# A memory layer's running sums as VectorE scans along the tokens, batch by batch, with the token dispatch interleaved

## The chip, the cores and the metric

The kernel runs on one core of a Trainium2 chip. The metric is the device time of one execution in microseconds. Engine names in the rows: PE is TensorE (PEld its weight loads), DVE is VectorE, ACT is ScalarE, POOL is GpSimd, SP is SyncE, which here only issues DMAs.

## What is computed

The input is `x` of 4 batches, 1024 tokens, 128 channels, in float32. Two layers follow each other, each with a residual and a layer norm.

```
z = x @ W_in                       # memory channels 128 + 32, query channels 256
z_mem = causal depthwise conv, 4 taps, of the first 160 channels
p   = exp(clip(score_scale * z_mem[128:160]) + log weight of the position)     # (b, l, 32)
phi = z_mem[0:128] * theta         # 32 heads k, 4 h, 8 m = 1024 features a token
num = cumsum over tokens of p * (cos phi, sin phi);  den = cumsum of p
y   = sum over m of num * query / max(den, 1e-4);  y = silu(y scaled) @ W_out
x1  = layernorm(x + y)
out = layernorm(x1 + sum over the 2 best of 8 experts of weight * mlp_e(x1) + mlp_shared(x1))
mlp(x) = square(relu(x @ w_up)) @ w_down       # 128 -> 512 -> 128
```

The cosine and sine of 4096 tokens by 1024 features, their weighting by `p`, their running sum over the tokens and the product with the query are the bulk of the first layer.

## The kernel before

**Memory stage.** A unit is 128 tokens of one batch, the tokens on the partitions; there are `NT` = 32 units, and unit `i` belongs to batch `i % 4`. `phases(i)` (L604) forms 1024 phases in PSUM; ScalarE rounds them (`rounding`, L383), VectorE takes the fraction (`fraction`, L748), ScalarE makes `Abs` and two sines (L387, L390, L394); the result is `feat`, 2 halves of 1024 columns. GpSimd multiplies each half by `p` (`weigh`, L495). The running sum within a unit is a matmul with the triangular matrix `tri` (`sums`, L620: 4 matmuls of 512 columns); what comes from the unit before of the same batch is carried by copying the last rows out of PSUM (`last_row`, L403) and adding them with an accumulating DMA into row 0 of the next `feat` (`carry`, L503). VectorE multiplies the sums with the query (`read_out`, L769) and reduces over `m` (L778, L787, L795). `value` (L543) is the convolution as 4 matmuls, `queries` (L590) the query projection.

**Dispatch stage.** It works on groups of 512 tokens, `NG` = 8 of them: transposing and projecting y (L938, L948), residual and statistics (`residual`, L1238 to L1246), `normalise`, transposing x1 (L959), router logits (`route`, L969), `choose` (L1266 to L1279), `rank`, `place` and `count` (each token's slot in the table), 8 indirect DMAs on GpSimd that write 128 rows each into the table in DRAM (`scatter`, L1192), and the shared MLP: `up` (L998, 4 matmuls of 512 columns a group), `relu` and `square` (L1116, L1122), `down` (L1008, 16 matmuls of 128 columns). Only the first group's front part runs beside the last units; the order of all of it is written out by hand in `rest()` of each engine.

**Routed and finish stages.** `routed` loads 46 tiles from the table (L1468), transposes them (L1488) and runs the experts' MLPs (L1500, L1513); `finish` adds, normalises and stores.

A float32 matmul leaves two MATMUL records in the trace (L620: 128 matmuls, 256 records); a transpose leaves one. Each engine executes its program in order and waits on semaphores in place.

## Time and profile before

| | us |
|---|---|
| median of 3 runs | 490.81 |
| lowest, highest run | 489.8, 494.01 |
| span of the profiled execution | 498.7 |
| PE busy in it | 453.9 |
| DVE busy | 356.7 |
| ACT busy | 354.5 |
| POOL busy | 315.1 |

The profiled execution's span is 7.9 us above the median of the runs. Busy times are sums over the whole span; the stages differ, so they are read by stretch. A granted clock (PEclk) of 1.00 is the higher of TensorE's two levels, 2.4 GHz, and 0.50 the lower, 1.2 GHz; values between are means over a stretch.

### The profile page before, as it was taken

The page shows a single profiled execution, that of the slowest core. Times are in us where ns is not written, and L with a number is a line of the kernel's source. Part 1 is how long each engine was busy: PE and PEld are TensorE (multiplying, and loading weights), DVE is VectorE, ACT ScalarE, POOL GpSimd, SP SyncE. Part 2 cuts the span into 40 slices and gives each one's busy share as a digit, 9 for nine tenths or more (in the row PEclk, how much of TensorE's full clock was granted, in tenths as well). Part 3 has the DMA queues.
Part 4 walks back from the last instruction along what each step waited for, and adds up shares of the span by engine and source line. Part 5 has one row for each costly group of instructions (what it writes and reads, how often), then busy time and mean ns, then how long its engine had stood idle before and what let it go on. Part 6 is the DMA issues. An engine that isn't in the chain of part 4 may idle for free.

```text
span 498.7 us, 7644 instructions
## 1 busy us (share of the span) xinstructions
PE 453.9 (91%) x2184; PEld 293.6 (59%) x2184; DVE 356.7 (72%) x873; ACT 354.5 (71%) x557; POOL 315.1 (63%) x285
## 2 busy tenths in 40 slices
PE   8997999999999988798898898489999999999983
PEld 5332444444344333455576675389999999899721
DVE  5898999999999999998688964353333333455246
ACT  3989999999999999815455555327667667566537
POOL 4754789999999999845566666604555455555421
PEclk9998999999999999989799999979999999999997
DMA  8031246654343434001111111131222222222095
GB/s 274 8 122 43 86 146 213 216 196 151 130 153 131 151 133 148 3 1 33 39 45 43 45 43 47 46 94 51 72 65 81 71 60 58 60 57 67 11 324 182
DMA packets 41193, 48.56 MB, mean 97 GB/s; under 512 B 5616, under 2 KB 25266, under 8 KB 41152
## 3 DMA queue, kind: packets, MB, share of 16 engines
q1 hardware_dynamic: 35792, 39.07, 23.8%
q0 software_dynamic: 5216, 8.70, 5.6%
q8 instruction: 18, 0.29, 0.2%
q10 hardware_dynamic: 144, 0.31, 0.2%
q14 instruction: 23, 0.19, 0.1%
HBM read 19.17 MB, written 29.11 MB: 97 GB/s over the span
## 4 chain that ended last, share of the span: by engine, by line
PE 40%; POOL 22%; DVE 16%; issue 8%; ACT 7%; DMA 2%; another core or an unknown queue 2%; DVEq 0%; POOLq 0%; SPq 0%; ACTq 0%
POOL memory_feat L495 17%; PE routed_ph L1500 13%; PE routed_po L1513 12%; PE dispatch_sph L998 4%; PE dispatch_spo L1008 3%; POOL memory_feat L503 2%; DVE memory_prod L769 2%; DVE memory_y_raw L778 2%; POOL memory_prod L518 2%; PE memory_nsum L620 1%; ACT finish_xo L1714 1%; PE routed_px L1488 1%; PE dispatch_plr L969 1%; DVE memory_feat L769 1%
## 5 line engine op out<-in xcount | busy, mean ns | idle before, releaser
L495 POOL TENSOR_TENSOR memory_feat<-memory_feat,memory_p_tok 128x1024 f32<-128x1024 f32 x64 | 125.9, 2063 | 17.1 <-ACT memory_feat L390 14.2
L620 PE MATMUL memory_nsum<-memory_feat,tri 128*128 128x512 f32 x256 | 118.1, 604 | 6.3 <-ACT memory_last_rows L403 2.4
L1476 POOL DMA_INDIRECT pick_scratch<-routed_ob,routed_xg x71 | 71.6, 1008 | 75.1 <-DVE routed_ob L1597 56.7
L1192 POOL DMA_INDIRECT table_scratch<-dispatch_xrow,dispatch_slot x64 | 61.9, 967 | 40.9 <-PE dispatch_sph L998 18.9
L620 PEld LDWEIGHTS memory_nsum<-memory_feat,tri 128*128 128x128 f32 x256 | 47.8, 192 | 65.1 <-issue 56.2
L1546 ACT ACTIVATE routed_rel<-routed_ph 128x512 f32<-128x512 f32 x71 | 42.3, 597 | 47.7 <-PE routed_ph L1500 46.7
L1513 PE MATMUL routed_po<-routed_w2c,routed_hid 128*128 128x128 f32 x568 | 71.3, 276 | 1.2 <-DVE routed_ob L1597 0.7
L1500 PE MATMUL routed_ph<-routed_xs,routed_w1c 128*128 128x256 f32 (+1 forms) x368 | 71.1, 337 | 1.2 <-DVE routed_w2c L1583 0.9
L1597 DVE TENSOR_SCALAR routed_ob<-routed_po,routed_xg 128x128 f32<-128x128 f32 x71 | 22.6, 347 | 69.2 <-issue 49.6
L769 DVE TENSOR_TENSOR memory_prod<-memory_nsum,memory_query 128x1024 f32<-128x1024 f32 x58 | 68.8, 1216 | 1.9 <-PE memory_nsum L620 1.8
L1513 PEld LDWEIGHTS routed_po<-routed_w2c,routed_hid 128*128 128x128 f32 x568 | 67.0, 192 | 1.9 <-issue 1.1
L1500 PEld LDWEIGHTS routed_ph<-routed_xs,routed_w1c 128*128 128x128 f32 x368 | 56.5, 191 | 6.2 <-ACT routed_xs L1537 1.8
L403 ACT COPY memory_last_rows<-memory_nsum 32x1024 f32<-32x1024 f32 x56 | 54.2, 1005 | 3.5 <-DVE memory_prod L769 2.6
L1116 ACT ACTIVATE dispatch_srel<-dispatch_sph 128x512 f32<-128x512 f32 x32 | 19.1, 596 | 38.4 <-PE dispatch_sph L998 29.8
L1008 PE MATMUL dispatch_spo<-w,dispatch_shid 128*128 128x128 f32 x256 | 36.0, 295 | 8.2 <-ACT dispatch_shid L1122 8.2
L1008 PEld LDWEIGHTS dispatch_spo<-w,dispatch_shid 128*128 128x128 f32 x256 | 34.4, 209 | 14.4 <-ACT dispatch_shid L1122 8.6
L1555 ACT ACTIVATE routed_hid<-routed_rel 128x512 f32<-128x512 f32 x71 | 42.5, 638 | 0.0
L748 DVE SCALAR_TENSOR_TENSOR memory_feat<-memory_feat,memory_ph 128x1024 f32<-128x1024 f32 x32 | 38.7, 1209 | 5.3 <-ACT memory_feat L383 4.5
L787 DVE TENSOR_REDUCE memory_y_raw<-memory_prod 128x96 f32<-128x1536 f32 x24 | 41.8, 1741 | 0.0
L604 PE MATMUL memory_ph<-setup_th_f,setup_k_val 64*128 64x512 f32 x128 | 36.8, 651 | 4.4 <-DVE memory_feat L748 4.4
L394 ACT ACTIVATE memory_feat<-memory_feat,memory_half_pi 128x1024 f32<-128x1024 f32 x32 | 36.5, 1140 | 0.0
L998 PE MATMUL dispatch_sph<-dispatch_x1T,w 128*128 128x512 f32 x64 | 35.0, 636 | 1.1 <-DVE memory_feat L769 1.1
(192 smaller groups left out, 694.6 us busy)
## 6 DMA issues: line engine op xcount, KB each, us to landing
table_scratch<-memory_blank SPq DMA_DIRECT2D x68, 260.0 KB, 2.6
finish_pick<-pick_scratch SPq DMA_DIRECT2D x16, 256.0 KB, 6.0
routed_xg<-table_scratch SPq DMA_DIRECT2D x25, 130.0 KB
w<-w_up SPq DMA_DIRECT2D x9, 256.0 KB, 2.7
w<-w_down SPq DMA_DIRECT2D x9, 256.0 KB, 3.1
x_tok<-x SPq DMA_DIRECT2D x4, 512.0 KB, 3.7
out<-finish_xo SPq DMA_DIRECT2D x7, 256.0 KB, 2.3
routed_xg<-table_scratch SPq DMA_DIRECT2D x21, 65.0 KB
```

The lines of the kernel that those rows point to most:

```text
L403: nc.scalar.copy(last_rows[32 * b:32 * b + 32, h * NF:(h + 1) * NF], nsum[96:P, h * NF:(h + 1) * NF]).then_inc(rows_kept, 1)
L495: nc.gpsimd.tensor_tensor(v, v, pv, ALU.mult).then_inc(wfeat_done, 1)
L620: last = nc.tensor.matmul(nsum[:, o:o + 512], tri[:], feat[:, i % U, h, q * 512:(q + 1) * 512], start=True, stop=True)
L769: nc.vector.tensor_tensor(products(i)[:, h, :].rearrange("p (q r c) -> p q r c", q=KQ, r=REP), nv, qv.unsqueeze(2).broadcast_to([P, KQ, RE ...
L998: nc.tensor.matmul(sph[q % 2][:], w1[:, E, q * P:(q + 1) * P], x1T[:, g % XR].rearrange("p t c -> p (t c)"), start=True, stop=True).then_i ...
L1008: last = nc.tensor.matmul(spo[g % 2][:, t * D:(t + 1) * D], shid[:, g % 2, q, t * P:(t + 1) * P], w2[:, E, q, :], start=(q == 0), stop=(q ...
L1192: nc.gpsimd.indirect_dma_start(out=table, in_=xrow[:, r, n, :], in_offset=None, out_offset=bass.IndirectOffsetOnAxis(ap=slot[:, r, n:n + 1 ...
L1476: nc.gpsimd.indirect_dma_start(out=pick_dram, in_=ob[:, u, h, :], in_offset=None, out_offset=bass.IndirectOffsetOnAxis(ap=xg[:, t % XU, h, ...
L1500: last = nc.tensor.matmul(ph[s][:, q * n:(q + 1) * n], w1c[:, u, q * P:(q + 1) * P], xs[:, s, 0:n], start=True, stop=True)
L1513: last = nc.tensor.matmul(po[:, h * D:(h + 1) * D], hid[:, s, q * n + h * P:q * n + (h + 1) * P], w2c[:, u, q, :], start=(q == 0), stop=(q ...
L1546: nc.scalar.activation(rel[:, n % 2, :], ph[s][:, o:o + FC * P], ACT.Relu).then_inc(rel_done, 1)
L1555: nc.scalar.activation(hid[:, s, o:o + FC * P], rel[:, n % 2, :], ACT.Square).then_inc(hid_done, 1)
```

## The change

`memory` and `dispatch` become one stage, `front`. A **unit** is now one of 8 head indices `n` of one batch: 128 features on the partitions (4 query groups by 4 h by 8 m), 1024 tokens along the columns, cosine and sine as two halves. There are again 32 units (`NU`), batch by batch. The tables that `phases` multiplies have 32 rows instead of 64.

The weight `p` is no longer multiplied into the features. The sums are kept relative to the current weight: with r(t) = p(t-1)/p(t), the recurrence s(t) = r(t) s(t-1) + feature(t) is one `tensor_tensor_scan` of 1024 elements a half (`cumulated`); r is spread from 32 heads to 128 partitions by 4 matmuls of 256 columns (`broadcast`) into the single PSUM buffer `abc`, and the factor p/den is applied to the result (`scaled`). The product with the query is GpSimd's (`product`), the sum over `m` is TensorE's (`gathered`, 8 matmuls of 256 columns into 4 column groups). ScalarE applies the silu to 2 units' result and issues 4 DMAs (`move`) that put it in place for the output projection. The triangular matmuls, the row copies, the carry DMAs, the query products and the reductions on VectorE and the transposes of y are gone; so are 5 warming matmuls at the start.

The loop runs over steps `s` = 0 to 42. In step `s` every engine does its part of units near `s` and, for each group `g`, stage k = s - BASE[g] of the dispatch: 0 project, 1 statistics, 2 normalise, transpose and route, 3 choose and rank with the first half of the shared MLP's up, 4 place with the second half, 5 and 6 down, 7 keep, with `scatter` in 4 to 7. A group's two tokens blocks belong to one batch, so groups 0 and 1 can follow batch 0, and so on. The dispatch uses one PSUM bank for its chain and one for its MLP, so an `up` waits for the `relu` before it. The core of the diff (the small functions of the dispatch, the constants' layout and the setup are left out):

```diff
+BASE = (10, 14, 18, 22, 26, 30, 34, 35)
+LAST = BASE[-1] + 8
...
+        feat = sb("feat", [P, U, 2, L])
...
+        ph = ps("ph", L)
+        abc = ps("abc", L)
+        yb = ps("yb", 512)
+        kq = ps("kq", 512)
+        d1 = ps("d1", 512)
+        d2 = ps("d2", 512)
+        chain_bank = [d1[:]] * (NG - 2) + [ph[:, 0:512], abc[:, 0:512]]
+        mlp_bank = [d2[:]] * (NG - 2) + [ph[:, 512:], abc[:, 512:]]
...
+        def kq_work(s):
+            b, n = s // REP, s % REP
+            if b == B - 1:
+                return ("c", b, n) if n < 2 else None
+            if n < 2:
+                return ("v", b + 1, n)
+            if n < 4:
+                return ("c", b, n - 2)
+            return ("q", b + 1, n - 4)
...
+            def move(n):
+                b, g = n // PAIRS, n % PAIRS
+                act.wait_ge(silu_done, n + 1)
+                if b >= 2:
+                    act.wait_ge(proj_done, 2 * (b - 1))
+                for q in range(QT):
+                    act.dma_start(yT[2 * QH * g:2 * QH * (g + 1), b % 2, q * QL:(q + 1) * QL],
+                                  y_pair[2 * QH * q:2 * QH * (q + 1), n % 2]).then_inc(y_moved[n % 2], 16)
...
+            for s in range(LAST):
+                for g in range(NG):
+                    if stage(g, s) == 7:
+                        keep_shared(g)
+                if s + 2 < NU:
+                    features(s + 2)
+                for g in range(NG):
+                    if stage(g, s) == 2:
+                        keep_x(g)
+                if s + 3 < NU:
+                    rounding(s + 3)
+                if s < NU:
+                    keep(s)
+                if 3 <= s <= NU + 1 and s % 2:
+                    silu((s - 3) // 2)
+                    move((s - 3) // 2)
+                for g in range(NG):
+                    k = stage(g, s)
+                    if k == 2:
+                        second_row(g)
+                    elif k == 3:
+                        weigh(g)
+                        hidden(g, 0)
+                        hidden(g, 1)
+                    elif k == 4:
+                        hidden(g, 2)
+                        hidden(g, 3)
...
+            def product(i, h):
+                b = i // REP
+                if i % REP == 0:
+                    pool.wait_ge(kq_kept, q_use(b, 2 * h + 1) + 1)
+                pool.wait_ge(scan_done, 2 * i + 1 + h)
+                v = feat[:, i % U, h]
+                nc.gpsimd.tensor_tensor(v, v, query[:, b % 2, h], ALU.mult).then_inc(prod_done, 1)
...
+            for s in range(LAST):
+                for g in range(NG):
+                    k = stage(g, s)
+                    if k == 1:
+                        inverse_root(g)
+                    elif 4 <= k < 8:
+                        scatter(g, k - 4)
+                if s < NU:
+                    product(s, 0)
+                    product(s, 1)
...
+            def value(bank, b, n):
+                for t in range(TAPS):
+                    last = nc.tensor.matmul(bank, wconv[:, t, n * KH // 2:n * KH // 2 + KH],
+                                            xT[:, b, n * HL + 1 + t:n * HL + 1 + t + HL],
+                                            start=(t == 0), stop=(t == TAPS - 1))
+                return last
+            def ask(b, n):
+                return nc.tensor.matmul(kq[:], wq[:, n // 2], xT[:, b, HALO + (n % 2) * HL:HALO + (n % 2 + 1) * HL],
+                                        start=True, stop=True)
...
+            def phases(i):
+                b, n = i // REP, i % REP
+                if i == 0:
+                    pe.wait_ge(k_first, 2)
+                else:
+                    pe.wait_ge(frac_done, i)
+                if n == 0 and b:
+                    pe.wait_ge(kq_kept, v_use(b, 1) + 1)
+                for h in range(2):
+                    q = (n // 2 + 2 * h) % QT * 2 * QH
+                    last = nc.tensor.matmul(ph[:, h * HL:(h + 1) * HL], th[q:q + 2 * QH, n].rearrange("p c m -> p (c m)"),
+                                            k_val[q:q + 2 * QH, b % 2, h * HL:(h + 1) * HL], start=True, stop=True)
+                last.then_inc(ph_done, 1)
+            def broadcast(i):
+                b, n = i // REP, i % REP
+                if n == 0:
+                    pe.wait_ge(rr_ready, min(b, 1) + 1)
+                if i:
+                    pe.wait_ge(scan_done, 2 * i)
+                def quarter(q):
+                    return nc.tensor.matmul(abc[:, q * QL:(q + 1) * QL],
+                                            spread[q * K:(q + 1) * K, n].rearrange("p c m -> p (c m)"),
+                                            rr[q * K:(q + 1) * K, b, 1:], start=True, stop=True)
+                quarter(0)
+                quarter(2).then_inc(abc_even, 1)
+                pe.wait_ge(abc_even, i + 1)
+                quarter(1)
+                quarter(3).then_inc(abc_done, 1)
+            def gathered(i):
+                n = i % 2
+                if n == 0 and i:
+                    pe.wait_ge(y_scaled, i // 2)
+                for h in range(2):
+                    pe.wait_ge(prod_done, 2 * i + 1 + h)
+                    for q in range(QT):
+                        last = nc.tensor.matmul(yb[2 * QH * q:2 * QH * (q + 1), 0:QL], gather[:, n],
+                                                feat[:, i % U, h, q * QL:(q + 1) * QL],
+                                                start=(n == 0 and h == 0), stop=(n == 1 and h == 1))
+                last.then_inc(red_done, 1)
...
+            for s in range(LAST):
+                if s < NU:
+                    broadcast(s)
+                if s + 3 < NU:
+                    phases(s + 3)
+                for g in range(NG):
+                    k = stage(g, s)
+                    if k == 0:
+                        project(g)
+                    elif k == 2:
+                        turn_x(g)
+                    elif k == 3:
+                        up(g, 0)
+                    elif k == 4:
+                        up(g, 2)
+                if s == 0:
+                    offsets()
+                if 0 < s <= NU:
+                    gathered(s - 1)
+                if s < NU:
+                    feed(s)
+                for g in range(NG):
+                    k = stage(g, s)
+                    if k == 2:
+                        route(g)
+                    elif k == 3:
+                        up(g, 1)
+                        rank(g)
+                    elif k == 4:
+                        up(g, 3)
+                    elif k == 5:
+                        down(g, (0, 1))
+                    elif k == 6:
+                        down(g, (2, 3))
+                if s == BASE[-1] + 4:
+                    total()
...
+            def cumulated(i):
+                dve.wait_ge(abc_done, i + 1)
+                for h in range(2):
+                    dve.wait_ge(feat_done, 2 * i + 1 + h)
+                    v = feat[:, i % U, h]
+                    nc.vector.tensor_tensor_scan(v, abc[:], v, 0.0, ALU.mult, ALU.add).then_inc(scan_done, 1)
+            def scaled(n):
+                b, g = n // PAIRS, n % PAIRS
+                dve.wait_ge(red_done, 2 * n + 2)
+                dve.wait_ge(kq_kept, c_use(b, g // 2) + 1)
                 if n >= 2:
+                    dve.wait_ge(y_moved[n % 2], 16 * QT * (n // 2))
+                nc.vector.tensor_tensor(y_pair[:, n % 2], yb[:, 0:QL], c_all[:, g], ALU.mult).then_inc(y_scaled, 1)
 
...
+            for s in range(LAST):
+                if s + 2 < NU:
+                    fraction(s + 2)
+                for g in range(NG):
+                    k = stage(g, s)
+                    if k == 4:
+                        place(g)
+                        count(g)
+                    elif k == 1:
+                        measure(g)
+                    elif k == 2:
+                        normalise(g)
+                    elif k == 3:
+                        choose(g)
+                if s == BASE[-1] + 4:
+                    table_of_tiles()
+                    table_of_halves()
+                if 3 <= s <= NU + 1 and s % 2:
+                    scaled((s - 3) // 2)
+                if s == 0:
+                    quarter_sums()
+                elif s == 1:
+                    keep_offsets()
+                    denominators(0)
+                    invert(0)
+                elif s == 2:
+                    ratios(1, B)
                     constants()
+                elif s % REP == 4 and s // REP + 1 < B:
+                    denominators(s // REP + 1)
+                elif s % REP == 5 and s // REP + 1 < B:
+                    invert(s // REP + 1)
```

The prologue on TensorE is, in order: `value` of the first half of batch 0's tokens, `scores(0)` (16 matmuls of 257 columns in 4 column groups), `value` of the second half, `scores(1)` to `scores(3)`, `phases(0)`, `ask(0, 0)`, `phases(1)`, `ask(0, 1)`, `phases(2)`, `ask(0, 2)`, `ask(0, 3)`. On ScalarE: the exponentials, `rounding(0)`, six more exponentials, a table load, then `keep_query`, `features(0)`, `keep_query`, `rounding(1)`, `keep_query`, `features(1)`, `keep_query`, `rounding(2)`.

## Rows read from the trace of the kernel before

**Rows 1.** busy time and granted clock by stretch (stretch; length, engines busy with counts, PEclk, DMA)
```profile
45.00:190.00 145.00, 142.09 (x387) 59.29 (x386) 140.97 (x135) 142.69 (x152) 127.46 (x96) 1.00 0.45 156
...
218.00:332.00 114.00, 94.89 (x545) 69.93 (x543) 80.46 (x393) 53.72 (x114) 62.91 (x65) 0.94 0.13 42
```

**Rows 2.** one timeline, 318 to 330 us cut in two stretches, same columns
```profile
318.00:324.00 6.00, 0.00 (x0) 0.00 (x0) 0.86 (x3) 0.95 (x2) 3.33 (x4) 0.87 0.14 43
...
324.00:330.00 6.00, 5.67 (x29) 5.67 (x30) 3.91 (x18) 0.28 (x1) 1.17 (x2) 0.56 0.23 65
```

**Rows 3.** VectorE groups by line and form (line, engine, operation, shapes, count | busy, mean ns | idle)
```profile
L748 DVE SCALAR_TENSOR_TENSOR memory_feat<-memory_feat,memory_ph 128x1024 f32<-128x1024 f32 x32 | 38.7, 1209 | 5.3 <-ACT memory_feat L383 4.5
...
L728 DVE TENSOR_TENSOR_SCAN setup_den<-setup_one_row,setup_pT 128x512 f32<-128x512 f32 x1 | 1.2, 1214 | 0.0
...
L1308 DVE TENSOR_TENSOR_SCAN dispatch_whole<-dispatch_one,dispatch_whole 128x8 f32<-128x8 f32 x1 | 0.2, 204 | 0.0
...
L739 DVE RECIPROCAL memory_inv_den<-memory_inv_den 128x128 f32<-128x128 f32 x8 | 7.5, 941 | 0.0
```

**Rows 4.** VectorE in order of time, from 31 us (start, length, engine, line, operation)
```profile
31.55 1.22 DVE L748 SCALAR_TENSOR_TENSOR memory_feat<-memory_feat,memory_ph 128x1024 f32<-128x1024 f32 x1
...
32.69 2.35 DVE L769 TENSOR_TENSOR memory_prod<-memory_nsum,memory_query 128x1024 f32<-128x1024 f32 x2
```

**Rows 5.** groups by line and form, TensorE
```profile
L543 PE MATMUL memory_pk<-memory_xT,memory_wconv 128*128 128x512 f32 x56 | 31.5, 652 | 0.0
...
L604 PE MATMUL memory_ph<-setup_th_f,setup_k_val 64*128 64x512 f32 x128 | 36.8, 651 | 4.4 <-DVE memory_feat L748 4.4
...
L998 PE MATMUL dispatch_sph<-dispatch_x1T,w 128*128 128x512 f32 x64 | 35.0, 636 | 1.1 <-DVE memory_feat L769 1.1
...
L1008 PE MATMUL dispatch_spo<-w,dispatch_shid 128*128 128x128 f32 x256 | 36.0, 295 | 8.2 <-ACT dispatch_shid L1122 8.2
...
L969 PE MATMUL dispatch_plr<-routerT,dispatch_x1T 128*128 128x8 f32 x64 | 9.0, 268 | 2.9 <-DVE dispatch_slot L1295 2.0 <-ACT dispatch_x1T L1099 0.5 <-issue 0.4
```

**Rows 6.** timeline of the first 8 us
```profile
1.46 4.16 PE L626 MATMUL memory_ph<-setup_one_row 128*128 128x256 f32 x10 [1.46 <-DVE setup_one_row L677]
...
2.55 0.43 SPq L322 DMA_DIRECT2D ident<-tabs  x1
...
3.02 0.44 SPq L323 DMA_DIRECT2D tri<-tabs  x1
...
5.80 1.13 PE L553 MATMUL memory_pq<-memory_xT,memory_wconv 128*128 128x128 f32 x8 [0.19 <-DMA memory_xT<-x_T]
...
6.87 0.64 PE L534 MATMUL memory_nsum<-memory_xT,setup_w_in 128*32 128x259 f32 x8
```

**Rows 7.** groups by line and form, ScalarE and GpSimd
```profile
L390 ACT ACTIVATE memory_feat<-memory_feat 128x1024 f32<-128x1024 f32 x32 | 33.6, 1049 | 0.0
...
L1122 ACT ACTIVATE dispatch_shid<-dispatch_srel 128x512 f32<-128x512 f32 x32 | 20.2, 632 | 0.8
...
L495 POOL TENSOR_TENSOR memory_feat<-memory_feat,memory_p_tok 128x1024 f32<-128x1024 f32 x64 | 125.9, 2063 | 17.1 <-ACT memory_feat L390 14.2 <-ACT memory_p_tok L363 2.7
```

**Rows 8.** timeline, one choice of experts on VectorE around 304 us
```profile
304.12 0.19 DVE L1266 COPY dispatch_lg<-dispatch_plr 128x32 f32<-128x32 f32 x1 [2.43 <-PE dispatch_plr L969]
...
305.77 0.19 DVE L1279 TENSOR_TENSOR dispatch_sel<-dispatch_hot 128x32 fp32r<-128x32 f32 x1
```

**Rows 9.** DMA issues of the carry (count, KB each, median us to landing)
```profile
memory_feat<-memory_last_rows POOLq DMA_DIRECT2D x28, 8.0 KB, 2.1
```

**Rows 10.** timeline where the dispatch ends and the routed stage begins
```profile
318.98 0.96 POOL L1192 DMA_INDIRECT table_scratch<-dispatch_xrow,dispatch_slot  x1 [0.30 <-issue]
...
324.55 0.95 POOL L1192 DMA_INDIRECT table_scratch<-dispatch_xrow,dispatch_slot  x1 [0.34 <-ACT dispatch_shid L1122]
...
327.14 8.43 SPq L1468 DMA_DIRECT2D routed_xg<-table_scratch  x8
...
330.34 0.38 PE L1488 MATMUL routed_px<-ident,routed_xg 128*128 128x128 f32 x2
```

1651 lines of the change are left out of this document (607 added, 1044 removed).

## The prediction

> **What bounds the kernel now.** I read the busy time by stretch first. In the memory stage three engines are full at once: of 145 us PE is busy for 142.1, VectorE for 141.0, ScalarE for 142.7, at the full clock; one unit takes 6.0 us [rows 1]. From 218 to 332 us the dispatch runs with PE at 94.9 of 114 us, VectorE at 80.5 and ScalarE at 53.7 [rows 1]: this is the room that running the dispatch beside the units is to use. The timeline of the stage's end gives the mark against which I sum: the last scatter starts at 324.55, the table is read from 327.14, the first transpose of the routed stage starts at 330.34 [rows 10]. What follows (168.4 us to the end of the 498.7) has the same instructions after the change, so I carry it over. The question is when that transpose starts.
>
> **Costs in the new stage.** Times here are from one start to the next: L748 starts at 31.55 and its successor at 32.69, 1.14 us for a record of 1.22 [rows 4].
> - Scan: 512 elements took 1.214 us, 8 took 0.204 [rows 3], so 1024 take 1.21 + 512 x 0.0020 = 2.24. Two with the overlap above: 4.4 us a unit. No row has a scan that reads PSUM. From below this is the bound; from above I add 0.1 for two, since L748 reads PSUM and takes 1.21 for 1024.
> - VectorE a unit: fraction 1.14, scans 4.4, every second step `scaled` about 0.35 (256 wide). Gone are the products and reductions, so a unit costs VectorE 5.7 instead of about 5.9. Nothing is won there, and the group work comes on top: choice 1.85 [rows 8], and at the same rate of small instructions, as estimates, statistics 1.5, normalise 2.0, place and count 1.15. A batch's `denominators` and `invert` add 1.0 and 2.0 (the reciprocal of 128 took 0.94 [rows 3], here 256).
> - PE: a 512-column matmul is two records, and 28 of them were busy for 31.5 us; in a row 0.86 to 0.9, alone 1.1 [rows 5]. `phases`: two row groups side by side took 36.8 / 32 = 1.15 [rows 5]. No row has 32-row operands; the nearest is that one, and the four 32-column groups of 259 columns, 8 records in 0.64 [rows 6]. So `broadcast` is two such pairs one behind the other, 1.4 with the semaphore between (1.0 to 2.0 as bounds), `gathered` 1.1 (1.0 to 2.1, if the column groups ran one by one), `value` 3.6, a factor or a query step 1.0. A group: project 2.0, turn 0.65, route 1.1 (9.0 / 8), up 4 x 0.95, rank 0.8, down 36.0 / 8 = 4.5 plus 0.3 net for its first matmul.
> - ScalarE: four activations of a unit, each a bit under 1.05 [rows 7], 4.0; a keep 0.5; group work 7. New on its queue: `move` issues 4 DMAs. An issue holds its queue: on SP they start at 2.55 and 3.02 [rows 6], 0.46 each, so 1.85 us in every second step. Below, 0, if ScalarE's queue ran on; that engine's constants were the only DMA it issued before, so I take 0.46.
> - GpSimd: two products at 2.0 [rows 7] and two scatters at 1.27 (0.96 and 0.30 before it [rows 10]) make 6.6 a step: never the bound.
>
> The Trainium skill (TensorE: Matmul & The Clock Gate, Part 3) measures four 32-row tiles at 3.07 times one and three 32-column tiles at 2.38, so packing is not free there. By that, as an estimate, `gathered` and `broadcast` would cost some 0.4 more a step and the sum below 8 more; 0.64 for four column groups [rows 6] speaks for the cheaper value.
>
> **The prologue.** Input is there at 5.80 [rows 6]. The warming matmuls are gone; they took 4.16 for work that at full clock takes half [rows 6], so the first `value` costs 5.2, not 3.6: 11.0. `scores(0)` 1.9, `value` 3.4, `scores(1)` to `(3)` 5.2, `phases(0)` 1.1: 22.6. Rounding 1.0; then ScalarE has six exponentials, a table load, a keep, `features(0)` 3.0, a keep, and only then `rounding(1)`: 32.2. Fraction, `phases(2)`, `ask(0, 2)`: 35.6. Keep, `features(1)`, keep, `rounding(2)`: 40.5. Fraction and quarter sums 2.3, scans 4.4: unit 0 ends at 47.2.
>
> **Steps 1 to 10.** `broadcast(s)` waits for both scans of s-1, since `abc` is one buffer, and the scan waits for it: 0.1 + 1.4 + 0.15 = 1.65 from scan to scan, of which the fraction hides 1.14. A light step is 1.65 + 4.4 = 6.1. Step 1 has the denominators (8.7), step 2 `ratios` over 768 columns and the constants (8.6), 3 is 6.1, 4 6.5, 5 7.9, 6 to 8 6.1 each; in step 8 and 9 PE carries a `value` of 3.6 between its broadcasts: 1.4 + 1.15 + 1.2 + 3.6 = 7.3, felt in 9 and 10. Sum 70.7. `project(0)` waits about 2 for the landing of the last `move` (the carry's DMA took 2.1 [rows 9]): unit 10 ends at 120.
>
> **Steps 11 to 31.** Now PE has 5.0 to 7.4 for the unit and 3.5 for its group, VectorE 5.7 and 1.6; whichever is later passes it on through `abc`. By stage of the group:
> - project steps (14, 18, 22): PE 1.4 + 1.15 + 2.0 + 0.9 + 1.2 + 1.0, then `up(g, 3)`, which waits for ScalarE's relu: 9.6 each, 28.8.
> - statistics (15, 19, 23): 1.4 + 1.15 + 1.2 + 1.0 + 2.8 = 7.6 each, 22.8.
> - normalise (12, 16, 20, 24): 8.5, 11.6 (with a `value`), 8.9, 8.9: 37.9.
> - choice (13, 17, 21, 25): ScalarE does features, rounding, keep (done 6.0 after the broadcast's start, 8.7 with a `value`), silu, `move` 1.85, weights 0.6, and only then the relu on which `up(g, 1)` and behind it `rank` and the next broadcast wait: 6.0 + 0.35 + 1.85 + 0.6 + 0.55 + 0.95 + 0.8 = 11.1, and 13.9 in 17: 47.2. VectorE alone would need 8 to 10 here.
> - step 11: 7.5; 26 to 31, with no feed: 7.6, 7.5, 8.0, 9.6, 7.6, 7.3: 55.1 together.
> Sum 191.8, mean 9.1; unit 31 ends at about 312.
>
> **The tail**, in us after that. Behind normalise(5) (2.0), the last gather (3.9), route(5) (7.0) and choose(5) (9.0) VectorE reaches the last `scaled`: 9.3. Silu and `move` to 11.7, landing 13.6; relu, up and rank of group 5 stand ahead of project(6) on PE: 16.9. Statistics 18.5; the power stands behind 4 scatters on GpSimd: 21.8; normalise(6) 23.9; `turn_x` waits behind down(5), route behind its second half: 28.2; choose(6) 30.1, normalise(7) 32.1, then relu, up, rank(6) 36.4 and place(6) 37.3. choose(7) 39.5, relu and up of both groups in turn, rank(7) 44.6, place(7) 45.5. Then 12 scatters x 1.27: 60.8. From the last scatter to the transpose it was 5.8 - 0.95 = 4.8 [rows 10]: 65.6.
>
> **The sum.** 312 + 65.6 = 377.4 against 330.3: +47 us. The profiled execution would be 546; the runs' median lies 7.9 below its profile, so 490.8 + 47 = 538. All engines' work shrinks a little, but units and groups now share engines that units already filled: 22 shared steps at 9.1 instead of 32 at 6.0 and a dispatch of 114, plus a prologue 17 longer and 2 groups left over.
>
> **Rivals.**
> 1. The forecast, a chain through `abc`, ScalarE's relu and a serial tail: 0.64. Its own range: ScalarE's issues at 0 take away 8 and overlaps that I walked too strictly as much again; the upper bounds of packing add 15: 515 to 555.
> 2. Not slower, through one mechanism: PE's and ScalarE's parts of a group all fit beneath VectorE, so that a step costs only VectorE's own time. Then steps 11 to 31 are 21 x 5.54, `scaled` 3.9, group work 34, denominators 6, together 160 instead of 192; with it ScalarE is never waited for, in the prologue (42) or in the tail (57). 42 + 72 + 160 + 57 = 331: 491. It decides from a mean of 7.6 a step, where my walk has 9.1. For it: GpSimd and ScalarE sum to under 7.5 a step. Against: PE's sum is 8.6 before any wait, and one bank for the chain and one for the MLP leave no slack. 0.15, of which faster by over 1% 0.09.
> 3. The clock falls. Before, the stretch with PE at 0.00 of 6 us was followed by one at 0.56 [rows 2], so a pause brings the 1.2 GHz level. PE now idles for 4 us in the prologue, in step 2 and repeatedly in the tail, and 1 to 1.5 in each light step. If steps 3 to 7 ran at half, PE would need 9.2 in them instead of 4.6, +15; a tail in part at half +8: 561. 0.12. The Trainium skill (TensorE: Matmul & The Clock Gate, Part 1) has an idle array fall to half rate and stay there until it has again been busy for a while. Taken so, the tail's +8 is sure and the light steps are open.
> 4. The packing fails (32-row and 32-column tiles one by one): `broadcast` 2.0 and `gathered` 2.1, +1.6 in 32 steps: 589. Against it: 0.64 [rows 6]. 0.02.
> The rest, 0.07, is a wait that I don't see, either way.
>
> **Range and chances.** 500 to 562 takes in 1, 3 and the upper edge of 2. 1% is what a measurement here can tell from no change: faster 0.09, within 1% 0.06, slower 0.85.
>
> **What would show it.** The transpose of the routed stage at 360 to 385 us; scans of 2.2 to 2.3 us, 64 of them; `broadcast` 1.4 to 1.6 from the scan's end; steps 13, 17, 21 and 25 the longest, with PE waiting for ScalarE's relu; unit 0 done at 47; 60 us or more from the last scan to the routed stage. I'd be wrong if PE is busy for under 80% of the shared steps without waiting for ScalarE, if the prologue ends by 40, or if ScalarE's DMA issues cost it nothing.

## The result, and the profile after

| | before | changed |
|---|---|---|
| median of the runs, us | 491.82 | 591.94 |
| lowest to highest | 489.8 to 494.01 | 590.25 to 597.57 |
| span of the profiled execution | 498.7 | 589.3 |
| mean granted clock | 0.974 | 0.843 |

The changed kernel takes 1.206 times as long (95% interval 1.199 to 1.213). The direction was forecast, the size was not: 592 lies 54 us above the forecast and above the range.

The page's first two parts for the changed kernel: busy time of each engine, then TensorE's clock in 40 slices.

```profile
PE 489.6 (83%) x2760; PEld 305.8 (52%) x2760; DVE 358.7 (61%) x772; ACT 313.8 (53%) x531; POOL 302.8 (51%) x223
...
PEclk9956876788869967969978777867699999999997
```

VectorE is busy for 358.7 us where it was 356.7: nothing was taken off it. I call steps 1 to 10, which hold units alone up to the first project, the light steps, steps 11 to 31, which hold a unit and a part of a group each, the shared steps, and what follows the last unit the tail. By stretch (start and end, length, busy time of PE, PEld, DVE, ACT and POOL with their instructions, then PE's granted clock, DMA share and GB/s), most of each of the three:

```profile
70.00:130.00 60.00, 50.96 (x237) 19.26 (x238) 51.34 (x33) 35.13 (x43) 38.16 (x17) 0.73 0.39 129
130.00:318.00 188.00, 156.10 (x852) 80.17 (x852) 145.00 (x245) 112.35 (x157) 118.62 (x72) 0.83 0.22 74
318.00:412.00 94.00, 73.44 (x361) 47.42 (x360) 45.91 (x172) 30.72 (x60) 50.80 (x42) 0.76 0.24 80
```

No stretch has an engine at 97 or 98%, as [rows 1] had three. In the shared steps VectorE has 77% and PE 83%, at a clock of 0.83. The groups that answer [rows 3, 5, 7], by line and form:

```profile
L896 DVE TENSOR_TENSOR_SCAN front_feat<-front_abc,front_feat 128x1024 f32<-128x1024 f32 x64 | 143.0, 2276 | 25.5 <-PE front_abc L683 25.4
L683 PE MATMUL front_abc<-front_rr,front_spread 32*128 32x256 f32 x256 | 54.8, 511 | 13.9 <-DVE front_feat L896 11.8
L769 PE MATMUL front_d<-front_x1T,front_w1s 128*128 128x512 f32 x48 | 37.3, 868 | 30.1 <-ACT front_srel L492 30.1
L889 DVE SCALAR_TENSOR_TENSOR front_feat<-front_feat,front_ph 128x1024 f32<-128x1024 f32 x32 | 38.4, 1201 | 20.8 <-ACT front_feat L445 20.8
L931 DVE TENSOR_TENSOR front_newton<-front_var,front_root 128x4 f32<-128x4 f32 x8 | 8.5, 1059 | 1.2 <-POOL front_root L593 1.2
```

The scan is as expected. Three waits stand out: PE for ScalarE's relu (30.1 us), VectorE for the broadcast (25.4), VectorE for the rounding (20.8). And 128x4 elements took 1.06 us on VectorE, where the same operation before took 0.18:

```profile
L1256 DVE TENSOR_TENSOR dispatch_newton<-dispatch_var,dispatch_root 128x4 f32<-128x4 f32 x20 | 3.6, 182 | 0.6
```

**Marks.** All comparisons below use four marks, read from the timelines: the end of the scans of unit 0, 10 and 31, and the start of the routed stage's first transpose. After that mark come 165 to 169 us in every kernel here (169.3 in the changed one, 168.4 in the one before).

| us | forecast | measured | difference |
|---|---|---|---|
| unit 0 | 47.2 | 51.2 | +4.0 |
| steps 1 to 10 | 72.8 | 79.6 | +6.8 |
| steps 11 to 31 | 191.8 | 214.0 | +22.2 |
| tail, from unit 31 to the transpose | 65.6 | 75.2 | +9.6 |
| transpose | 377.4 | 420.05 | +42.6 |

The transpose of the changed kernel:

```profile
420.05 0.69 PE L1192 MATMUL routed_px<-ident,routed_xg 128*128 128x128 f32 x2 [7.17 <-DMA routed_xg<-table_scratch]
```

### The profile page after: what moved, and what is told of

The parts are those of the page before. It is cut to its first block, busy times and chain, and to the rows that moved or that the text cites. A ratio compares the mean times of both kernels' runs of the same rounds, so it can differ in the third digit from the quotient of the medians.

```text
span 589.3 us, 8472 instructions
## 1 busy us (share of the span) xinstructions
PE 489.6 (83%) x2760; PEld 305.8 (52%) x2760; DVE 358.7 (61%) x772; ACT 313.8 (53%) x531; POOL 302.8 (51%) x223
## 4 chain that ended last, share of the span: by engine, by line
PE 62%; DVE 15%; ACT 8%; issue 5%; ACTq 4%; DMA 3%; POOL 2%; SPq 1%; DVEq 0%; POOLq 0%
PE routed_ph L1204 11%; PE routed_po L1217 11%; DVE front_feat L896 6%; PE front_d L769 5%; PE front_abc L683 5%; PE front_yb L699 4%; ACTq L466 4%; PE front_ph L671 3%; PE front_kq L629 3%; PE front_d L780 2%; DVE front_feat L889 2%; PE front_kq L635 2%; POOL table_scratch L602 2%; PE front_abc L629 2%; PE front_d L722 2%
## 5 line engine op out<-in xcount | busy, mean ns | idle before, releaser
L589 POOL TENSOR_TENSOR front_feat<-front_feat,front_query 128x1024 f32<-128x1024 f32 x64 | 149.4, 2354 | 116.3 <-DVE front_feat L896 116.0
L896 DVE TENSOR_TENSOR_SCAN front_feat<-front_abc,front_feat 128x1024 f32<-128x1024 f32 x64 | 143.0, 2276 | 25.5 <-PE front_abc L683 25.4
L602 POOL DMA_INDIRECT table_scratch<-front_xrow,front_slot x64 | 63.0, 985 | 64.2 <-DVE front_slot L976 46.9
L1301 DVE TENSOR_SCALAR routed_ob<-routed_po,routed_xg 128x128 f32<-128x128 f32 x71 | 22.6, 348 | 74.9 <-PE routed_po L1217 74.8
L683 PE MATMUL front_abc<-front_rr,front_spread 32*128 32x256 f32 x256 | 54.8, 511 | 13.9 <-DVE front_feat L896 11.8
L769 PE MATMUL front_d<-front_x1T,front_w1s 128*128 128x512 f32 x48 | 37.3, 868 | 30.1 <-ACT front_srel L492 30.1
L889 DVE SCALAR_TENSOR_TENSOR front_feat<-front_feat,front_ph 128x1024 f32<-128x1024 f32 x32 | 38.4, 1201 | 20.8 <-ACT front_feat L445 20.8
L450 ACT ACTIVATE front_feat<-front_feat 128x1024 f32<-128x1024 f32 x32 | 33.7, 1052 | 31.0 <-DVE front_feat L889 15.9
L671 PE MATMUL front_ph<-front_k_val,front_th 32*128 32x512 f32 x128 | 44.4, 776 | 5.7 <-DVE front_feat L889 5.7
L699 PE MATMUL front_yb<-front_feat,front_gather 128*32 128x256 f32 x512 | 41.8, 453 | 0.7 <-DVE front_y_pair L904 0.7
L453 ACT ACTIVATE front_feat<-front_feat,front_half_pi 128x1024 f32<-128x1024 f32 x32 | 36.3, 1133 | 0.0
L769 PEld LDWEIGHTS front_d<-front_x1T,front_w1s 128*128 128x128 f32 x48 | 9.4, 245 | 47.2 <-ACT front_srel L492 36.4
L451 ACT ACTIVATE front_feat<-front_feat 128x1024 f32<-128x1024 f32 x32 | 33.3, 1041 | 0.0
```

The costliest lines, as they stand in the source:

```text
L589: nc.gpsimd.tensor_tensor(v, v, query[:, b % 2, h], ALU.mult).then_inc(prod_done, 1)
L602: nc.gpsimd.indirect_dma_start(out=table, in_=xrow[:, k, g % XG, t, :], in_offset=None, out_offset=bass.IndirectOffsetOnAxis(ap=slot[:, k, ...
L671: last = nc.tensor.matmul(ph[:, h * HL:(h + 1) * HL], th[q:q + 2 * QH, n].rearrange("p c m -> p (c m)"), k_val[q:q + 2 * QH, b % 2, h * HL ...
L683: return nc.tensor.matmul(abc[:, q * QL:(q + 1) * QL], spread[q * K:(q + 1) * K, n].rearrange("p c m -> p (c m)"), rr[q * K:(q + 1) * K, b ...
L699: last = nc.tensor.matmul(yb[2 * QH * q:2 * QH * (q + 1), 0:QL], gather[:, n], feat[:, i % U, h, q * QL:(q + 1) * QL], start=(n == 0 and h ...
L769: nc.tensor.matmul(mlp_bank[g], w1s[:, q * P:(q + 1) * P], x1T[:, g % 2].rearrange("p t c -> p (t c)"), start=True, stop=True).then_inc(up ...
```

## The experiments

Every kernel with its marks; "21 steps" is from unit 10 to unit 31, and the clock is the mean of the profiled execution. Where a kernel leaves work out, its expectation says which.

| run | median us | ratio to before | unit 0 | unit 10 | unit 31 | 21 steps | tail | clock |
|---|---|---|---|---|---|---|---|---|
| changed kernel | 591.94 | 1.206 | 51.2 | 130.8 | 344.8 | 214.0 | 75.2 | 0.843 |
| e1_fill | 588.01 | 1.193 | 49.4 | 128.0 | 347.1 | 219.1 | 74.5 | 0.918 |
| e2_move_sp | 569.58 | 1.158 | 51.3 | 129.4 | 328.7 | 199.3 | 71.8 | 0.871 |
| e3_half_scan | 573.51 | 1.168 | 48.1 | 120.0 | 324.9 | 204.9 | 76.2 | 0.856 |
| e4_fill_move | 564.87 | 1.147 | 51.9 | 129.5 | 323.4 | 193.9 | 70.2 | 0.939 |
| e6_no_mlp | 571.82 | 1.165 | 51.3 | 131.0 | 337.5 | 206.5 | 64.3 | 0.795 |
| e7_hoist | 557.56 | 1.132 | 51.1 | 129.2 | 318.1 | 188.9 | 69.6 | 0.885 |
| e9_hoist_fill | 559.19 | 1.138 | 53.3 | 132.0 | 319.1 | 187.1 | 73.3 | 0.922 |
| e17_hoist_short_product | 534.15 | 1.088 | 50.7 | 124.4 | 295.5 | 171.1 | 66.5 | 0.896 |
| e18_hoist_link | 553.73 | 1.127 | 51.6 | 124.1 | 316.3 | 192.2 | 68.5 | 0.857 |
| e5_apart | 609.68 | 1.240 | 50.7 | 131.5 | 280.3 | 148.8 | 156.9 | 0.847 |
| e10_apart_fill | 620.47 | 1.267 | 51.2 | 129.9 | 271.8 | 141.9 | 177.2 | 0.949 |
| e11_apart_link | 601.40 | 1.226 | 49.9 | 127.8 | 275.3 | 147.5 | 156.4 | 0.827 |
| e12_apart_half | 591.17 | 1.205 | 47.9 | 119.6 | 261.2 | 141.6 | 157.5 | 0.869 |
| e13_units_sp | 602.69 | 1.226 | 51.1 | 129.1 | 277.6 | 148.5 | 156.5 | 0.850 |
| e14_units_sp_link | 581.95 | 1.185 | 51.6 | 124.1 | 255.3 | 131.2 | 156.2 | 0.840 |
| e15_units_sp_tap | 598.38 | 1.218 | 51.2 | 127.2 | 271.7 | 144.5 | 156.3 | 0.833 |
| e16_units_all | 577.32 | 1.176 | 50.4 | 122.7 | 252.7 | 130.0 | 156.4 | 0.829 |

Four theories were weighed: **clock** (PE at 1.2 GHz), **ScalarE's queue** (issues and activations ahead of the relu), **scans** (VectorE bound), and, later, **contention** between VectorE and GpSimd.

### The clock, ScalarE's queue, and the scans (e1 to e4)

e1 adds matmuls that write columns nobody reads, where PE would idle:

```diff
+            def fill(bank, n):
+                for _ in range(n):
+                    nc.tensor.matmul(bank[:, 258:512], flat[:, 0:128], flat[:, 0:254], start=False, stop=True,
+                                     skip_group_check=True)
...
+                        fill_free(s, 3)
                         up(g, 1)
...
+                fill_free(s, 2 if s < NU else 4)
```

> All the computation of the changed kernel, plus idle-time matmuls on TensorE that nobody reads (254 columns each, into a PSUM range that is free at that moment): 5 at the start, 3 between the prologue's query steps, 2 at the end of a step, 3 ahead of a choice step's second up, 4 at the end of each tail step. In the changed kernel 1.2 GHz was granted in 18 stretches, together some 180 of the 420 us before the routed stage. Theory A (the pauses bring the low clock, and the low clock is what made the steps 10.2 us instead of 9.1 and prologue and tail longer): the mean granted clock goes from 0.84 to 0.93 or more and the time falls by 25 to 45 us, to 547 to 567. Theory B (the waits for ScalarE are the cost, the clock follows but costs little): the clock rises, the time stays within 8 us of 592, since the added matmuls stand in the waits. Theory C (the scan chain on VectorE bounds the steps): no change or slower by up to 10.

e2 takes the four DMA issues of `move` from ScalarE and gives them to SyncE, behind its wait for the scans of the step:

```diff
                     silu((s - 3) // 2)
-                    move((s - 3) // 2)
...
+                if 3 <= i <= NU + 1 and i % 2:
+                    move(s, (i - 3) // 2)
```

> All the computation. The 64 small DMAs of move go from ScalarE's queue to SP's; nothing else changes. In the changed kernel the four of a choice step hold ScalarE for 2.4 us ahead of the relu that TensorE's second up waits for, and TensorE then stands still for 4.5 us. Theory B (that wait is the cost): 8 choice steps shorter by 2.4 each and some shorter light steps, 20 to 30 us less, more if the pause it ends also kept the clock down (to 550). Theory A alone: under 10 us, for other pauses still bring the low clock. Theory C: nothing.

e3 scans half of the tokens, and e4 is e1 and e2 together:

```diff
-                    nc.vector.tensor_tensor_scan(v, abc[:], v, 0.0, ALU.mult, ALU.add).then_inc(scan_done, 1)
+                    nc.vector.tensor_tensor_scan(v[:, 0:HL], abc[:, 0:HL], v[:, 0:HL], 0.0, ALU.mult, ALU.add
+                                                 ).then_inc(scan_done, 1)
```

> Leaves out the running sums of the second 512 tokens (the scans take only the first half of the columns), so VectorE's scans cost 1.2 us each instead of 2.28: 2.2 us less in each of 32 units. Theory C (VectorE's scans bound the steps): about 65 us less, to 527. Theory A or B (TensorE, its clock and its waits bound them): only the light steps 1 to 7 and parts of others get shorter, 5 to 25 us less; the granted clock does not fall.

> All the computation; both edits of the runs before: idle-time matmuls and move on SP's queue. Theory A and B together: the gains overlap in the choice steps; 40 to 60 us less, to 532 to 552, mean granted clock 0.95 or more. If it comes out at the better of the two alone, the clock was lost only through the choice steps' pause.

Raising the mean clock from 0.84 to 0.92 gave 4 us (e1), and on top of e2 4.7 (e4), where 532 to 552 us in all had been expected. With e1's matmuls the 21 steps got longer, 219.1 us instead of 214.0. So the added matmuls give only a lower bound on the clock's price. Where they lift the clock in a step that PE holds, the price is plain. The three project steps (14, 18, 22), from the start of one unit's broadcast to the start of the next's, took 12.2, 11.6 and 12.8 us in the changed kernel, at a clock of 0.68 to 0.76. They took 13.3, 11.8 and 12.7 in e1, which left the clock there at 0.69 to 0.78, and 12.5, 12.0 and 12.8 in e2, but 9.9, 9.4 and 9.9 in e4, at 1.00. Step 14 in the changed kernel, in e2 and in e4:

```profile
165.69:177.89 12.20, 10.96 (x46) 4.41 (x45) 8.41 (x19) 6.15 (x8) 8.96 (x7) 0.72 0.17 61
161.50:174.03 12.53, 11.29 (x45) 4.71 (x44) 9.57 (x19) 6.15 (x8) 10.13 (x8) 0.70 0.27 97
159.59:169.44 9.85, 8.61 (x48) 3.94 (x47) 9.68 (x16) 5.67 (x7) 7.95 (x6) 1.00 0.34 126
```

That is 8.2 us between e2 and e4 in three steps, and e4's added matmuls give about half of it back in the statistics and normalise steps (61.8 us in e2, 65.8 in e4, by the same measure). Halving the scans takes 64 x 1.07 = 68 us of scans off VectorE and only 18 off the kernel, 9 of them in the 21 steps: scans don't set the shared steps. Giving the issues away takes 22.4 us off. The choice step of the changed kernel shows the mechanism, ScalarE first, then PE:

```profile
158.79 0.42 ACT L458 ACTIVATE front_y_pair<-front_y_pair 128x256 f32<-128x256 f32 x1
159.24 2.44 ACTq L466 DMA_DIRECT2D front_yT<-front_y_pair  x4
161.73 0.21 ACT L481 ACTIVATE front_ratio<-front_gap 128x4 f32<-128x4 f32 x1 [2.52 <-issue]
...
162.18 0.58 ACT L492 ACTIVATE front_srel<-front_d 128x512 f32<-128x512 f32 x1
...
162.81 2.07 PE L769 MATMUL front_d<-front_x1T,front_w1s 128*128 128x512 f32 x2 [4.53 <-ACT front_srel L492]
```

The 4 issues took 2.44 us, 0.61 each, not the 0.46 of [rows 6]. The relu at 162.18 stands behind them, PE waits 4.53 us for it, and then runs the next matmuls at half clock (0.50 from 162.8 to 172.5): 2.07 for the two records that took 1.12 to 1.13 in other steps. The project step behind it starts with that clock, waits 1.17 us more for a relu, and passes the delay on to VectorE:

```profile
179.40 4.47 DVE L896 TENSOR_TENSOR_SCAN front_feat<-front_abc,front_feat 128x1024 f32<-128x1024 f32 x2 [3.76 <-PE front_abc L683]
```

### The dispatch behind the units, and without its MLP (e5, e6)

e5 moves every group behind the last unit; e6 keeps the changed kernel's order:

```diff
-BASE = (10, 14, 18, 22, 26, 30, 34, 35)
+BASE = (34, 38, 42, 46, 50, 54, 58, 62)
...
-        yT = kept_sb("yT", [P, 2, L])
+        yT = kept_sb("yT", [P, B, L])
```

> All the computation, with the dispatch taken apart from the units again: its first group starts in step 34, one group every 4 steps, after all 32 units (the transposed y holds 4 batches instead of 2, the shared MLP's hidden buffer one group instead of 2). It separates the price of the units from that of the groups between them. Theory A/B (the groups' waits and pauses make the shared steps 10.2 us): steps 11 to 31 take 6.3 to 7.3 each, unit 31 ends at 265 to 285 instead of 345; the dispatch alone then takes some 17 to 20 us a group, so the whole is 600 to 640: interleaving does pay for itself, and the loss against the kernel before lies in the serial tail and in units no faster than before. Theory C' (the turned memory stage itself is slow, whatever stands between): steps 11 to 31 stay above 9.

```diff
-                nc.scalar.activation(srel[:, q % 2], mlp_bank[g], ACT.Relu).then_inc(rel_done, 1)
+                nc.scalar.activation(srel[:, q % 2, 0:8], mlp_bank[g][:, 0:8], ACT.Relu).then_inc(rel_done, 1)
...
```

(Square, `up` and `down` are cut to 8 columns in the same way.)

> Leaves the shared MLP's arithmetic out: its up and down matmuls, relu and square work on 8 columns instead of 512 (and down is one matmul a token block instead of four), with all waits as they were. About 8 us of TensorE work and 4 us of ScalarE work a group are gone. If TensorE's own work bounds the shared steps, they go from 10.2 to about 8.5 us and the tail shrinks by 10: 540 to 555. If the waits and the clock bound them, the pauses get longer and the granted clock lower, and the gain stays under 20 us: 572 or more.

Units alone take 7.1 us a step (148.8 / 21) where the old stage had 6.0 [rows 1], and the whole dispatch behind them 156.9. Run beside each other, the same work ends at 420 instead of 437: the interleaving, which this change is about, is worth 17 us. That is its worth with the issues on ScalarE's queue: with them on SyncE's it is 33 (569.6 in e2 against 602.7 in e13, below), since the issues cost the shared steps 14.7 us and the units alone 0.3. Removing nearly all of the MLP's work takes 7.5 us off the 21 steps and 10.9 off the tail, 20 in all, so its engine time isn't most of what fills a shared step. The clock of the 21 steps fell with it, from 0.83 to 0.73, which can hide a part of the gain.

### The relus early (e7), the kernel before again (e8), and the clock once more (e9)

e7 is e2 with ScalarE's first relu and square of a choice and of a place step ahead of the rounding:

```diff
+                for g in range(NG):
+                    if stage(g, s) in (3, 4) and g < NG - 1:
+                        hidden(g, 0 if stage(g, s) == 3 else 2)
                 if s + 3 < NU:
                     rounding(s + 3)
```

> All the computation. move on SP's queue as in e2_move_sp, and in a choice and a place step ScalarE runs the first relu and square of the shared MLP right after the sines, ahead of the rounding and the kept copies, so that TensorE's second up no longer waits for what feed produces late in the step. Theory B (waits for that relu): another 8 to 20 us less than e2_move_sp's 569.6, 550 to 562, with choice steps at 9 instead of 10 to 11. If TensorE's work or the scan's wait for the broadcast bound these steps, within 4 us of e2_move_sp.

> The kernel before once more, for its profiled span: it was 498.7 us against a median of 491.8, while the changed kernel's profile lies 2.6 below its median. If profiling costs this kernel 7 us, the span is 497 to 500 again; if that one execution was an outlier, it is 488 to 494. The first would make 9 of the 54 us by which the forecast fell short an error of method (adding a difference of spans to a median).

A further 12.0 us. PE's list of waits (us in total, times, longest) shows the cause, in the changed kernel and in e2; in e7 0.9 us are left of it:

```profile
PE front_d L769 <- ACT front_srel L492: 30.1, 9, 5.3
```

```profile
PE front_d L770 <- ACT front_srel L494: 14.6, 10, 2.6
```

e7 is the fastest version that does all the work, at 1.132 times the kernel before (1.128 to 1.136). e8's span is 490.0, its transpose starts at 322.4: the profile that I summed against (330.3, 498.7) was longer than any run since.

e9 is e7 with e1's matmuls only in the prologue, the light steps and the tail, where PE waits:

> The changed kernel with the move's DMAs on SyncE's queue and the relus early (the edit that gave 557.6 us, E10 = 129.2, last scan at 318.1, tail 69.6), and with idle-time matmuls on PE only where no step of a group runs: five at the start, three behind each query and phase step of the prologue, three at the end of each of steps 0 to 9, four at the end of each step of the tail; they write columns that nobody reads. Earlier the idle-time matmuls also stood ahead of up(g, 1) and in the feed, where PE was itself late. Theory clock (PE at 1.2 GHz makes each broadcast up to 1.4 us longer while VectorE waits for it): the clock of steps 1 to 9 goes from 0.73 to over 0.9, their end from 129.2 to 122, the tail from 69.6 to 64: about 545. Theory chain (the clock is low because PE waits, and costs little): at most 4 us, 554 to 558.

The clock of the light steps rose from 0.81 to 0.91 and their end didn't move forward (132.0 against 129.2); the whole is 1.6 us slower, which is within the runs' spread. So the clock of the light steps is not what carries the cost; the project steps stand outside of this test, since e9 adds nothing in them. A single light step does show a price, at the low clock (changed kernel) and at the high one (e10, below):

```profile
71.63 2.51 PE L683 MATMUL front_abc<-front_rr,front_spread 32*128 32x256 f32 x8 [5.93 <-DVE front_feat L896]
...
74.19 4.47 DVE L896 TENSOR_TENSOR_SCAN front_feat<-front_abc,front_feat 128x1024 f32<-128x1024 f32 x2 [1.17 <-PE front_abc L683]
```

```profile
186.87 1.47 PE L682 MATMUL front_abc<-front_rr,front_spread 32*128 32x256 f32 x8 [0.79 <-DVE front_feat L917]
```

2.51 against 1.47 for a broadcast, 7.1 against 6.2 for the step (6.0 for e10's shortest). PE had waited 5.93 us before the slow one. In a light step the clock takes about 1 us where a scan waits for the broadcast; a project step, with more of PE's work in it, lost 2.6 to 3.0 (e2 against e4).

### What holds a unit by itself (e10 to e16)

These keep the dispatch behind the units, so the 21 steps hold nothing but units. e10 adds the idle-time matmuls; e11 and e12 remove a link and half of the scans:

```diff
             def broadcast(i):
                 b, n = i // REP, i % REP
-                if n == 0:
-                    pe.wait_ge(rr_ready, min(b, 1) + 1)
+                if n:
+                    return
+                pe.wait_ge(rr_ready, min(b, 1) + 1)
```

> The layout in which the whole dispatch follows the last unit (609.7 us, last scan at 280.3, TensorE's clock 0.71 from 130 to 280), with the same idle-time matmuls: five at the start, three behind each query and phase step of the prologue, three at the end of each unit's step, four a step afterwards. Here nothing but the units runs in steps 0 to 31, so the price of the clock in a unit can be read: theory clock, units at 6.1 to 6.5 us each instead of 7.4, the last scan at 255 to 262, 585 to 592 in all; theory chain, the clock rises over 0.9 and the last scan stays above 275.

> The same layout without idle-time matmuls, and the broadcast of the ratios made only for the first unit of each batch; the other 28 units' scans read what stands in abc (left out: 28 of 32 broadcasts, so the sums of those units are of other heads' weights). It takes away the link scan, broadcast, scan through the one buffer abc. Theory chain: a unit falls from 7.4 to VectorE's own 5.7 to 5.9, the last scan from 280 to 235 to 245. If ScalarE (four activations, a keep and half a move, 6.0 a unit) or PE at the low clock is just behind, a unit stays above 6.5 and the last scan above 255.

> The same layout, broadcasts whole, with the scans only over the first 512 of a unit's 1024 tokens (left out: the running sums of the other 512 tokens). VectorE has 2.2 us less a unit. Theory scans (the scan stands in series with the broadcast, so each us less of it is a us less of a unit): 7.4 falls to 5.2, if ScalarE's 6.0 lets it to 6.0: the last scan at 238 to 245. Theory that PE at the low clock or ScalarE binds a unit: above 6.6 a unit, the last scan above 258.

e10: 141.9 instead of 148.8 for the 21 steps, at a clock of 0.93 instead of 0.78 between 130 and 230 us. So the clock costs a unit about 0.33 us, at least: more than the chain theory allowed (a last scan above 275; it was 271.8) and less than the clock theory forecast (255 to 262). The same matmuls lengthen the dispatch by 20 us, where PE is then busy for 166 of 177 us. e11: my expectation of 235 to 245 missed, the last scan stood at 275.3. e12: 6.7 a step and the last scan at 261.2, as the rival to the scans had it: PE or ScalarE is right behind VectorE, and the run doesn't tell which. In e11 something else took the link's place. ScalarE and then VectorE of that kernel:

```profile
182.75 0.60 ACT L420 ACTIVATE front_k_val<-front_kq 128x512 f32<-128x512 f32 x1 [3.51 <-PE front_kq L627]
183.24 0.41 ACT L458 ACTIVATE front_y_pair<-front_y_pair 128x256 f32<-128x256 f32 x1
183.68 2.44 ACTq L464 DMA_DIRECT2D front_yT<-front_y_pair  x4
...
189.12 1.00 ACT L445 ACTIVATE front_feat<-front_ph 128x1024 f32<-128x1024 f32 x1
```

```profile
190.15 1.22 DVE L888 SCALAR_TENSOR_TENSOR front_feat<-front_feat,front_ph 128x1024 f32<-128x1024 f32 x1 [4.70 <-ACT front_feat L445]
```

ScalarE stands 3.51 us for the `value`, then issues for 2.44, then owes the sines and the rounding: VectorE waits 4.70 us. Four runs take these links away one by one and together. e13 has SyncE's issues (e2's edit); e14 has them and one broadcast a batch; e15 has them, a broadcast for each unit, and one tap of four:

```diff
-                for t in range(TAPS):
+                for t in range(TAPS if b == 0 else 1):
```

and e16 all three.

> The layout with the dispatch after the units (609.7 us; from the end of unit 10's scans to that of unit 31's 148.8 us, 7.1 a step), with the move's DMAs issued by SyncE instead of ScalarE. Theory ScalarE (its queue of four activations, a keep, a silu and 2.44 us of issues each second step holds the fraction, and so the unit): 21 steps take 134 to 140, the whole 595 to 602. Theory PE (value and broadcast at the low clock hold the unit): 145 to 149, 606 to 610.

> As the one with SyncE's issues and the units apart, and the broadcast made only for the first unit of each batch (left out: 28 of the 32 broadcasts). With ScalarE's issues in place this gave 147.5 us for the 21 steps instead of 148.8. Theory ScalarE: the issues hid the link, and now it shows: 120 to 126 us, 5.7 to 6.0 a step. Theory PE, through the value and the keep behind it: the steps with a value stay at 7.5 to 8 and the 21 steps at 134 or more.

> As the one with SyncE's issues and the units apart, the broadcasts whole, and the value of batches 1 to 3 made with one tap of the convolution instead of four (left out: three of four taps of the 6 values in the loop, 2.8 us of PE each at the full clock). Theory PE: the steps that carry a value fall from 8 to 6.2, 8 us or more in the 21 steps (4 of the 6 values lie there). Theory ScalarE: at most 3 us, as the value is hidden behind ScalarE's work.

> All three: issues on SyncE, one broadcast a batch, one tap in the loop's values. If these are all the links, VectorE alone is left, with 5.54 for fraction and scans, half of 0.4 for the scaling and the inverse of two batches (5.6 us each by the trace): 21 steps take 130 at the most and 122 at the least, and no light step is over 5.8. If another link holds (ScalarE's 5.0 a unit without the issues, or the ring of features), the light steps stay over 6.

| 21 steps of units alone, us | ScalarE issues | SyncE issues |
|---|---|---|
| a broadcast for each unit | 148.8 (e5) | 148.5 (e13) |
| one a batch | 147.5 (e11) | 131.2 (e14) |

Either link alone is worth 0.3 or 1.3 us; both together 17.6. Two chains run side by side, and each hides the other. (Theory ScalarE was wrong on e13, which moved only 0.3 in these steps. On e14 neither was met: 131.2 lies between its 120 to 126 and the other's 134.) The taps are worth 4.0 with the broadcasts, between the two theories again, and 1.2 without. VectorE's list of waits, 130 to 275 us, in e5 and then in e13, shows the swap (us in total, times, longest):

```profile
DVE front_feat L894 <- PE front_abc L681: 13.7, 13, 2.6
DVE front_feat L887 <- ACT front_feat L445: 5.0, 6, 1.5
```

```profile
DVE front_feat L895 <- PE front_abc L682: 20.6, 14, 3.6
```

With all three gone 130.0 us are left, 6.2 a step, at the upper end of what was expected, and four of the steps without a batch's extra work are over the 5.8 expected for them (7.2, 6.1, 6.5, 6.5). VectorE is busy for 117.7 of 120 us:

```profile
130.00:250.00 120.00, 80.84 (x433) 25.78 (x432) 117.72 (x75) 81.27 (x97) 90.27 (x40) 0.70 0.32 112
```

That is close to the floor of this design on VectorE. Nineteen steps of 5.54, two of 4.4 (30 and 31 have no fraction), 11 scalings of 0.4 and twice 4.6 for a batch's denominators and inverse make 128, 6.1 a step. It is no less than the 6.0 of the old stage [rows 1], before any link is counted.

### Contention, and the link in the shared steps (e17, e18)

```diff
-                nc.gpsimd.tensor_tensor(v, v, query[:, b % 2, h], ALU.mult).then_inc(prod_done, 1)
+                nc.gpsimd.tensor_tensor(v[:, 0:32], v[:, 0:32], query[:, b % 2, h, 0:32], ALU.mult).then_inc(prod_done, 1)
```

> The changed kernel with SyncE's issues and the early relus (557.6 us; from unit 10 to unit 31 188.9 us), with GpSimd's products made on the first 32 of 1024 columns (left out: the query product of the other columns). In that kernel between 130 and 320 us VectorE's first step of the root took 2.35 us for 128x4 in six groups, the addition to the variance 0.88, the product with the hot rows 0.93 for 128x64, the copy of the slots 0.53 for 128x8, where its neighbours of like size take 0.16 to 0.23. Theory contention (these wait while GpSimd's product of two SBUF operands runs): they fall to 0.15 to 0.3, some 22 us less of VectorE's time in the shared steps, the last scan from 318 to 300 or earlier, 540 or less. Rival (their length is their own, or they wait for the power on GpSimd): lengths stay, and the last scan moves by less than 5 us.

> The same kernel with whole products, and the broadcast made only for the first unit of each batch (left out: 28 of 32 broadcasts). Theory link (the scan, broadcast, scan link through abc holds the shared steps too): 188.9 us for the 21 steps fall by 17 or more, as in the units alone with SyncE's issues (148.5 to 131.2); 538 or less. Theory group (VectorE's own group work and PE's order of up, relu, rank hold them): less than 8 us, 548 or more.

e18: the 21 steps don't get shorter without the broadcasts (192.2 against 188.9; 3.8 us over the whole kernel come from the light steps). The link that bound the units binds no shared step: theory group.

e17: 23.4 us. Small groups of VectorE by line and form, in e7 (130 to 320 us) and then in e17 (130 to 300):

```profile
L937 DVE TENSOR_TENSOR front_newton<-front_var,front_root 128x4 f32<-128x4 f32 x6 | 14.1, 2352 | 0.0
...
L931 DVE TENSOR_SCALAR front_var<-front_mv 128x4 f32<-128x4 f32 x6 | 5.3, 876 | 0.2
L979 DVE TENSOR_TENSOR front_hit<-front_base,front_hot 128x64 f32<-128x64 f32 x5 | 4.7, 930 | 0.2
```

```profile
L937 DVE TENSOR_TENSOR front_newton<-front_var,front_root 128x4 f32<-128x4 f32 x6 | 0.9, 153 | 0.0
...
L979 DVE TENSOR_TENSOR front_hit<-front_base,front_hot 128x64 f32<-128x64 f32 x5 | 1.2, 239 | 0.2
```

The shared steps fell from 188.9 to 171.1. One instance in the changed kernel shows what happens, VectorE and then GpSimd:

```profile
184.90 1.56 DVE L931 TENSOR_TENSOR front_newton<-front_var,front_root 128x4 f32<-128x4 f32 x1
```

```profile
181.77 4.67 POOL L589 TENSOR_TENSOR front_feat<-front_feat,front_query 128x1024 f32<-128x1024 f32 x2 [2.98 <-DVE front_feat L896]
```

VectorE's four columns end at 186.46, GpSimd's pair of products at 186.44. It is so each time: all 9 of VectorE's 128x4 operations over 0.5 us in the changed kernel (130 to 345 us) and all 11 in e7 (130 to 320) end within 0.04 us after the end of a product. The small instruction doesn't run slowly; it waits inside its own record for the product to end. The Trainium skill (SBUF — State Buffer, "Who interferes with whom") says that VectorE with two SBUF inputs, or in a two-port mode, and a GpSimd operation that reads SBUF exclude each other for a whole instruction; the trace agrees, with 2.35 us beside the products and 0.15 without. The scans, with one input in PSUM, kept their 2.28 us in all kernels.

e17 also makes GpSimd's products end sooner, and with them what waits for a product, so not every microsecond of the 23.4 need be the contention. VectorE's busy time in five small groups (the three rows of e7 above, the copy of the slots and the difference of the two best logits) fell from 28.6 us in e7 to 4.9 in e17, and its last scan moved by 22.6.

## Why the prediction was wrong

**What held.** The costs of single operations: the scan 2.276 us (forecast 2.2 to 2.3), the broadcast 1.47 at full clock (1.4), `gathered` 1.07 (1.1), a light step 6.0 at full clock (6.1). VectorE gained nothing. PE waits for ScalarE's relu in the choice steps, behind `move`. That the units and groups share engines which units already filled, so that the interleaving brings little, is what e5 measured: 17 us against a serial order, with the issues where they are.

**The reference, +11.4.** I summed against a profile with its transpose at 330.3 and a span of 498.7, then took off 7.9 because the median lay below it. The changed kernel's median lies 2.6 above its span, which makes 10.5, and the stages after the transpose were 0.9 longer: 11.4 of the 54. The second profile of before (490.0, transpose at 322.4) shows that its extra 8 us lay ahead of the transpose, and belonged to that one execution. This is an error of method. Without it the forecast is about 548, and the 42.6 us up to the transpose remain.

**The prologue, +4.0.** The first `value` took 6.40 us from 6.59, not 5.2 from 5.80: six of its eight records took 1.06 us, where those of the second `value` took 0.59. That is 2.0. The other 2.0 are `phases(2)` and `ask(0, 2)`, priced at about 1.1 and 1.0, which ran at a clock of 0.50 after a pause of PE (here the first):

```profile
35.43 2.08 PE L671 MATMUL front_ph<-front_k_val,front_th 32*128 32x512 f32 x4 [3.52 <-DVE front_feat L889]
```

**Steps 1 to 10, +6.8.** Of it, steps 1, 2 and 4 have +1.4, +1.6 and +1.5. They are the ones with two SBUF operands on VectorE (denominators, `ratios`). In e17, with the products short, they took 8.9, 8.8 and 6.6 us: my 8.7, 8.6 and 6.5. The 128x256 scan of the denominators in step 1 shows it, first in the changed kernel, then in e17:

```profile
52.45 1.94 DVE L879 TENSOR_TENSOR_SCAN front_cc<-front_pw,front_offs 128x256 f32<-128x256 f32 x1
51.94 0.75 DVE L885 TENSOR_TENSOR_SCAN front_cc<-front_pw,front_offs 128x256 f32<-128x256 f32 x1
```

So the failed step here is the price of these operations, taken as if VectorE ran alone. Steps 3, 5, 7 and 8 have +1.0, +1.2, +1.5 and +1.2. Step 3 is the low clock's 7.1 of above, which I gave a chance of 0.12 and which is there in part of the light steps. Steps 5 and 7 took 7.9 and 6.0 in e2, as forecast, so theirs belong to the issues. Against that, step 10 took 2.3 less than forecast: PE's wait for the landing (3.00 us), which I had put ahead of unit 10, fell behind it, into step 11.

**Steps 11 to 31, +22.2.** Here is the step that failed: PE's walk through the shared steps. It is read best on PE, from the start of one broadcast to the start of the next, since a late PE delays the scan of the step behind:

| us | forecast | changed kernel | e2 | e4 | e7 |
|---|---|---|---|---|---|
| step 11 | 7.5 | 6.0 | 6.0 | 6.0 | 6.0 |
| normalise (12, 16, 20, 24) | 37.9 | 38.0 | 37.6 | 39.1 | 46.3 |
| choice (13, 17, 21, 25) | 47.2 | 53.0 | 41.1 | 41.2 | 35.1 |
| project (14, 18, 22) | 28.8 | 36.7 | 37.4 | 29.1 | 27.5 |
| statistics (15, 19, 23) | 22.8 | 24.2 | 24.2 | 26.7 | 20.9 |
| 26 to 30 | 40.3 | 44.8 | 41.5 | 40.8 | 41.7 |

The largest miss is the project step, priced at 9.6 with every matmul at the full clock. It took 11.6 to 12.8 at a clock of 0.68 to 0.76, and 9.4 to 9.9 where the clock was 1.00 (e4), with an idle-time matmul in it. I had let the clock fall in light steps and in the tail alone. The choice step comes next, priced at 11.1 and 13.9. In step 13 the relu came 9.6 us after the broadcast's start, not 8.8, of which the issues have 0.6 (0.61 each, not 0.46), and `up` and `rank` behind PE's wait of 4.53 us took 2.9 at the low clock, not 1.75. Without the issues (e2) the 21 steps take 14.7 less, where my bound was 8 for the whole kernel. The 0.46 was the row of another DMA: SyncE's issues of these same four take 2.42 in e2. I had given it a lower bound of 0 and no upper one. The normalise and statistics steps were right to 1.5 together. Their small operations are slowed by the products too (L931 took 1.36 us each from 130 to 345 us), but in the changed kernel PE's waits hide it. It shows once these are gone: the normalise steps took 46.3 us in e7 and 34.7 in e17. The remaining 4 us are step 10's, where `project(0)` waited 3.00 us for the landing and then ran at half clock. Steps 26 to 30 took 4.5 more, of which 3.3 are gone without the issues (e2).

**The tail, +9.6.** Without the issues and with the relus early it was 69.6 (e7), so 5.6 belongs to ScalarE's order; the rest was not separated (the clock was 0.72 there).

**The rivals.** "The clock falls" described what the records show, but put it in the wrong steps. What added matmuls win back on the whole is small: the medians of e1, e4 and e9 moved by -4, -5 and +2 against their own counterparts. These are lower bounds, since the matmuls cost time themselves. In the project steps alone the price is 8 us (e2 against e4), and e10 bounds it at 7 or more in 21 units. The clock's whole share of the 54 stays open. "All beneath VectorE" is what e16 made of the units, with work left out; in the full kernel it did not occur. Contention between VectorE and GpSimd wasn't among my rivals; in e7's order its price is at most some 23 us. What remains open: in the changed kernel's own order the removal of contention wasn't run, only in e7's. There the small groups are longer (28.6 us of busy time in the shared steps, against 15.1 in the changed kernel and 4.9 with short products), so in the changed kernel it can explain about 4 us of steps 1 to 10. Of the 22.2 it should explain little, since the normalise steps, where most of it stands, came out as forecast; no run shows this.

## What to carry over

When work moves from a stage of its own to one beside another, re-price its smallest instructions against the new neighbours, above all VectorE's with two SBUF operands beside GpSimd: here 128x4 elements went from 0.18 us to 2.35, the mean of six. Price the matmuls behind a wait of PE at the lower of the two clocks: three steps priced at 9.6 us took about 12.2. Taking away one of two parallel chains shows nothing; remove both before calling either harmless. And take the reference mark from more than one profile, when its span is 8 us above the median.

## What the runs showed of the hardware

- Four DMA issues of 32 rows of 1 KB held ScalarE's queue for 2.44 us in 13 of 16 places (2.48, 2.55 and 3.78 in the others). The same four on SyncE's queue took 2.41 or 2.42 in 13 of 16 places of e2, and ScalarE's own issues of constants started 0.45 and 0.49 us apart in the changed kernel. So the time of an issue went with the transfer, not with the engine.
- A VectorE addition to 128x4 elements took 0.88 us beside the products and 0.22 without, a cast of 128x8 0.53 and 0.17: not only operations with two tensor inputs wait.
- Keeping PE busy where it idles raised the granted clock (0.84 to 0.92, 0.81 to 0.91) and gained 4 us and nothing: the added matmuls also stand in PE's queue ahead of the ones that are needed, and in the dispatch by itself they cost 20 us. They paid where they kept the clock up in a step that PE held: 12.5, 12.0 and 12.8 us became 9.9, 9.4 and 9.9.
